# A two-layer sequence kernel: rows of B and C in 32-row groups, two Vector operations moved to GpSimd, and a new order of calls

## The reference

```
x = LN(x + gated recurrence(x))     # conv 4 taps, two gates, a scan of the log decay
                                    # clipped at -80, a scan of the state, out projection, rms norm
x = LN(x + W2 relu(W1 x + b1) + b2) # 256 -> 1024 -> 256
x = LN(x + SSM(x))                  # in projection -> x_in, z; conv 4 taps, silu;
                                    # (B, C, dt) = x_conv @ x_proj_w.T   (16 + 16 + 1 columns)
                                    # h[n] = exp(dt*A[n])*h[n] + dt*B[n]*x_conv   for 16 states n
                                    # y = sum over n of h[n]*C[n];  y*silu(z) @ out_proj_w.T
x = LN(x + W2 relu(W1 x + b1) + b2) # 16 experts of 64, which is one 256 -> 1024 -> 256
```

## Time and profile before

| | us |
|---|---|
| median of 3 runs | 961.66 |
| lowest and highest | 961.19 and 963.65 |
| the profiled execution | 961.2 |
| its span in the trace | 959.4 |

### The profile page before, as it was taken

How to read it: one execution, slowest core, us unless ns; L and a number is a source line. 1 busy time by engine, 2 the same in 40 slices (tenths; PEclk the granted TensorE clock), 3 DMA queues, 4 the chain that set the end, 5 groups by cost and what they waited for, 6 DMA issues and landing times. The chain is left out here.

```text
span 959.4 us, 9608 instructions
## 1 busy us (share of the span) xinstructions
PE 796.9 (83%) x2802; PEld 528.2 (55%) x2802; DVE 802.2 (84%) x1013; ACT 671.6 (70%) x1345; POOL 561.4 (59%) x468
## 2 busy tenths in 40 slices
PE   2385867978987799999899999998998797787585
PEld 1264644736554556475647564756476546546464
DVE  5245566677799999999999999999999999989761
ACT  4347687588767865997699769876976685465452
POOL 0202457437836793789378937893776376565421
PEclk9597977989998889999999999999999799789597
DMA  9000000000100010001000100010000000000000
GB/s 315 12 23 22 23 1 22 1 1 0 56 1 0 1 42 13 0 1 59 8 1 1 60 1 0 1 46 0 1 1 27 1 1 1 23 0 1 22 1 22
DMA packets 10341, 19.49 MB, mean 20 GB/s; under 512 B 1457, under 2 KB 5297, under 8 KB 10289
## 3 DMA queue, kind: packets, MB, share of 16 engines
q1 hardware_dynamic: 10288, 18.88, 5.8%
HBM read 14.69 MB, written 4.19 MB: 20 GB/s over the span
## 5 line engine op out<-in xcount | busy, mean ns | idle before, releaser
L385 POOL TENSOR_TENSOR y<-y,hC 128x1024 f32<-128x1024 f32 (+3 forms) x140 | 280.1, 2001 | 77.3 <-DVE hC L1461 73.4
L1914 PE MATMUL pC<-w,hT 128*128 128x256 f32 x1024 | 232.4, 382 | 4.9 <-ACT hT L754 4.9
L819 ACT ACTIVATE dA<-dt,A_neg 128x512 f32<-128x512 f32 (+3 forms) x320 | 187.5, 630 | 54.3 <-DVE hs L1450 53.8
L1914 PEld LDWEIGHTS pC<-w,hT 128*128 128x128 f32 x1024 | 194.5, 191 | 36.7 <-issue 7.2
L1450 DVE TENSOR_TENSOR_SCAN hs<-dA,carry,pS 128x512 f32<-128x512 f32 (+3 forms) x192 | 193.4, 1008 | 18.1 <-ACT dA L819 10.4
L2037 PE MATMUL pS<-stack,sel 97*128 97x512 f32 (+3 forms) x320 | 148.0, 515 | 54.5 <-DVE hs L1450 54.0
L1435 DVE TENSOR_TENSOR pS<-u,pS 128x1024 f32<-128x1024 f32 (+3 forms) x160 | 159.8, 999 | 17.4 <-PE pS L2037 16.8
L1461 DVE TENSOR_TENSOR hC<-hs,pS 128x1024 f32<-128x1024 f32 (+3 forms) x160 | 157.5, 985 | 15.3 <-PE pS L2037 15.1
L1450 DVE TENSOR_TENSOR_SCAN hs<-dA,pS 128x512 f32<-128x512 f32 (+1 forms) x128 | 138.2, 1080 | 14.6 <-POOL carry L392 6.0
L754 ACT ACTIVATE hT<-pA,ffb_sb 128x512 f32<-128x512 f32 (+3 forms) x160 | 94.7, 599 | 59.2 <-PE pA L1907 58.9
L1907 PE MATMUL pA<-tg,w 128*128 128x512 f32 (+3 forms) x320 | 127.9, 538 | 7.7 <-ACT hT L754 6.3
(11 more groups left out here) (120 smaller groups left out, 1101.5 us busy)
## 6 DMA issues: line engine op xcount, KB each, us to landing
xt<-xT SPq DMA_DIRECT2D x6, 515.0 KB, 4.7
xtok<-x SPq DMA_DIRECT2D x6, 512.0 KB, 5.3
out<-x3b SPq DMA_DIRECT2D x6, 512.0 KB, 2.9
w<-w1a SPq DMA_DIRECT2D x1, 1024.0 KB, 8.3
w<-w2a SPq DMA_DIRECT2D x1, 1024.0 KB, 10.4
w<-w1b SPq DMA_DIRECT2D x1, 1024.0 KB, 8.3
w<-w2b SPq DMA_DIRECT2D x1, 1024.0 KB, 9.9
xt<-xT SPq DMA_DIRECT2D x2, 259.0 KB, 7.8
```

The lines of the kernel that those rows point to most:

```text
L385: nc.gpsimd.tensor_tensor(y[:, :, 0:ch.T], so_far, hC[:, n % CRING, :, 0:ch.T], ALU.add).then_inc(S["y_sum"], 1)
L819: nc.scalar.activation(dA[:, k % ARING, 0:ch.T], dt[ch.side][:, h, 0:ch.T], ACT.Exp, scale=A_neg[:, h, n:n + 1]).then_inc(S["dA_ready"], 1)
L1914: mm = nc.tensor.matmul(dst[:, b * D:b * D + D], src(k, t0), w[:, k, :], start=k == 0, stop=k == nk - 1)
```

## The change

1. `x_proj` now yields 66 rows: two copies of B on partitions 0 to 31, two of C on 32 to 63, two of dt on 64 and 65. The weight for it is loaded once and laid out by three small copies on POOL (`x_proj_weights`). A column `hi_lo`, made from the identity at the start, tells on each row whether it is the rounded part or the remainder, so that `x_proj_high` and `x_proj_low` each work on all 66 rows.
2. A spread of B now multiplies 32 rows (0 to 31), one of C 32 rows (32 to 63), one of dt 2 rows. In PE's lists spread_B(n+2) and spread_C(n) stand directly next to each other nearly everywhere.
3. `decay_steps` and `readout` run on POOL. The factor 0.5 of the read-out moves into `op_w`, when it is centred.
4. All the lists of calls are in a new order. No other call is added or removed.

```diff
-                for at in (0, LO):
-                    weight("xp", xp_w[:, :, at:at + NX], xpT)
+                weight("xp", xp_in[:], xpT)
...
+            def decay_steps(ch):
+                c = ch.i
+                pool.wait_ge(S["la_scan"], 2 * c + 2)
+                nc.gpsimd.tensor_tensor(decay[:, :, 0:ch.T], st[:, 0:H, 1:1 + ch.T], st[:, 0:H, 0:ch.T], ALU.subtract).then_inc(S["dl_ready"], 1)
+
+            def readout(ch, gate):
+                if gate is not None:
+                    conv_done(pool, gate)
+                pool.wait_ge(S["y_sum"], ADDS * (ch.i + 1))
+                nc.gpsimd.tensor_tensor(yg[:, :, 0:ch.T], y[:, :, 0:ch.T], zz[ch.side][:, :, 0:ch.T], ALU.mult).then_inc(S["yg_ready"], 1)
+
+            def x_proj_weights(ch):
+
+                if ch.i == 0:
+                    pool.wait_ge(weight_loaded["xp"], 16)
+                    twice = xp_w[:, :, 0:DT_ROW].rearrange("p h (g r n) -> p h g r n", g=2, r=2)
+                    for k in range(2):
+                        nc.gpsimd.tensor_copy(twice[:, :, :, k, :], xp_in[:, :, 0:2 * NS].rearrange("p h (g n) -> p h g n", g=2)).then_inc(S["xp_ready"], 1)
+                    nc.gpsimd.tensor_copy(xp_w[:, :, DT_ROW:NXK], xp_in[:, :, 2 * NS:NX].to_broadcast([P, H, 2])).then_inc(S["xp_ready"], 1)
...
-                nc.scalar.mul(stack[ch.side][0:NXK, 0:ch.T], pA[0][0:NXK, 0:ch.T], 0.5).then_inc(S["stack_hi"], 1)
+                nc.scalar.activation(stack[ch.side][0:NXK, 0:ch.T], pA[0][0:NXK, 0:ch.T], ACT.Copy, scale=hi_lo[0:NXK, 1:2]).then_inc(S["stack_hi"], 1)
...
-                V.scalar_tensor_tensor(out=s[LO:NXK, 0:ch.T], in0=pA[0][LO:NXK, 0:ch.T], scalar=0.5, in1=s[LO:NXK, 0:ch.T].bitcast(F32),
-                                       op0=ALU.mult, op1=ALU.subtract).then_inc(S["stack_ready"], 1)
+                V.scalar_tensor_tensor(out=s[0:NXK, 0:ch.T], in0=pA[0][0:NXK, 0:ch.T], scalar=hi_lo[0:NXK, 0:1],
+                                       in1=s[0:NXK, 0:ch.T].bitcast(F32), op0=ALU.mult, op1=ALU.add).then_inc(S["stack_ready"], 1)
...
-            def spread(dst, ch, row):
-
-                return nc.tensor.matmul(dst[:, 0:ch.T], sel[0:NXK, row:row + 1].to_broadcast([NXK, P]), stack[ch.side][0:NXK, 0:ch.T],
+            def spread(dst, ch, lo, n, col):
+                return nc.tensor.matmul(dst[:, 0:ch.T], sel[lo:lo + n, col:col + 1].to_broadcast([n, P]), stack[ch.side][lo:lo + n, 0:ch.T],
                                         start=True, stop=True)
...
-                spread(pA[0], ch, 2 * NS).then_inc(S["s_mm"], 1)
+                spread(pA[0], ch, DT_ROW, 2, NS).then_inc(S["s_mm"], 1)
...
-                spread(B_bank(n), ch, n).then_inc(S["B_mm"], 1)
+                spread(B_bank(n), ch, 0, GROUP, n).then_inc(S["B_mm"], 1)
...
-                spread(C_bank(n), ch, NS + n).then_inc(S["C_mm"], 1)
+                spread(C_bank(n), ch, GROUP, GROUP, n).then_inc(S["C_mm"], 1)
```

More of the change, by code:

```diff
@@ L490, in entry @@
                 if scan is not None:
-                    save_carry(scan, 14)
                     sum_states(scan, 13)
@@ L529, in step @@
                     mconv_add(prep, 3)
+                if scan is not None:
+                    save_carry(scan, 7)
                 if gate is not None:
@@ L2129, in entry @@
                     if scan.i > 0:
-                        spread_B(scan, 2)
+                        spread_B(scan, 3)
+                if prep is not None:
+                    down(0, prep, 1, 1)
+                if gate is not None:
+                    gate_mm(gate, 1, 0)
+                if scan is not None:
+                    if scan.i > 0:
+                        spread_C(scan, 1)
+                if tail is not None:
+                    out_proj1(tail, prep)
+                if scan is not None:
+                    if scan.i > 0:
+                        spread_B(scan, 4)
+                        spread_C(scan, 2)
@@ new lines, in entry @@
+                if prep is not None:
+                    dt_row(prep)
+                if tail is not None:
+                    down(1, tail, 0, 0, gate=gate, prep=prep)
+                    down(1, tail, 0, 1)
+                if scan is not None:
+                    spread_B(scan, 13)
+                    spread_C(scan, 11)
+                if gate is not None:
+                    x1_transpose(gate, 0, prep, tail)
+                    x1_transpose(gate, 1, prep, tail)
+                if scan is not None:
+                    spread_B(scan, 14)
+                    spread_C(scan, 12)
@@ new lines, in entry, with step @@
+                if scan is not None:
+                    spread_C(scan, 14)
+                if prep is not None:
+                    spread_B(prep, 0)
+                if gate is not None:
+                    down(0, gate, 0, 0, tail=tail)
+                if scan is not None:
+                    spread_C(scan, 15)
+                if gate is not None:
+                    down(0, gate, 0, 1)
+            def step(ahead, gate, prep, scan, tail):
+                if scan is not None:
+                    spread_B(scan, 1)
+                if prep is not None:
+                    down(0, prep, 1, 0)
+                if scan is not None:
+                    spread_B(scan, 2)
+                    spread_C(scan, 0)
@@ L2151, in entry @@
                     x2_transpose(prep, 1, gate)
+                if scan is not None:
+                    spread_B(scan, 5)
+                    spread_C(scan, 3)
                 if tail is not None:
@@ L2169, in entry @@
                     up(1, tail, 1, prep)
+                if scan is not None:
+                    spread_B(scan, 7)
+                    spread_C(scan, 5)
                 if prep is not None:
+                    in_proj_z(prep, 0, tail)
                     in_proj_z(prep, 1, tail)
```

1215 lines of the change are left out of this document (571 added, 644 removed).

## The result

| | before | changed |
|---|---|---|
| median us (4 runs each) | 961.54 | 974.14 |
| lowest and highest | 961.19, 963.65 | 971.10, 978.73 |
| ratio, 95% interval | | 1.0137, 1.0095 to 1.0179 |
| profiled execution, its span | 961.2, 959.4 | 978.73, 976.9 |

What follows compares the result with a forecast made beforehand. DVE and PE together were taken to bound the late part of a step, DVE alone the early part. 961.2 - 13.2 + 6 x (0.4 - 0.25) + 1.2 + 1.5 = 951.6, 952 on the median's basis; range 944 to 974.

Steps and rivals of the forecast that it cites:

- the price of a pair: Spreads on PE: two neighbouring spreads taken at 0.23 us, against 0.43 for two now; bounds 0.22 to 1.5.
- the rival: Late part of a step, x_proj to C0: the switch costs more than the pass saved, 970 to 980 us; chance 0.20.
- the gap of over 0.5 us around a pair: Sign on PE that the forecast is wrong: a gap of over 0.5 us around each pair.
- single waits of 2 us: Sign that the forecast is wrong: DVE waits 2 us and more for spreads before output(12) and output(0).
- What leaves DVE: Read-out and difference of the decays leave DVE: 2.27 us a step of 512 tokens, 13.2 us in the bound stretch.
- What POOL gets: Two operations of 2.37 us a step on POOL, the difference starting when log_A ends, no stall; bounds nothing or 2.05 a step.
- What the new order asks of PE: Late part of a step: C12 1.2 us late, C0 1.8 at 0.43 a pair; 0.4 a step at 0.23, against 0.25 now.
- The ends: Tail +1.2 us for the last two read-outs; start +1.5, with bounds of -4 and +4.
- POOL once in each step: Rival: POOL shuts DVE out once in each step, 6 x 2.05 us on the sum, 964; chance 0.05.
- the order gains: Rival: the order gains by itself in the first 265 us, 4 to 8 us less, 945; chance 0.08.
- No more than two spreads: Rival: a pair costs 0.43 us, 1.8 late a step, +8.4, 960; chance 0.19 together with pairs in between.

Runs made afterwards that it cites:

- e10: Changed kernel (32-row spreads) with the opening and entry-step orders of before, difference of the decays placed where its input is ready; 967.88 us (1.0079).
- e8: Changed kernel with 97-row spreads and the opening and entry-step orders of before, difference of the decays placed where its input is ready; 951.57 us (0.9898).
- e5: Changed kernel, layout and order kept, each spread's matmul reading all 66 rows with zeros in the selection for the other groups; 961.43 us (0.9995).
- e3: Kernel before with only the 32-row layout of the spreads, order of before, both operations still on DVE; 976.02 us (1.0155).
- e1: Changed kernel with the 97-row layout of the spreads back, new order and move to POOL kept; 958.71 us (0.9961 of before).
- e11: 97-row spreads, old opening and entry orders, new step and closing order, with the two moved operations back on DVE; 968.86 us (1.0071).
- e7: Kernel before with only the two operations moved to POOL, decay_steps ahead of row_scales(LN_Y) in a step and of sum 2 in entry steps; 961.01 us (0.9975).
- e2: Kernel before with only the two operations moved to POOL, decay_steps queued late, behind row_scales(LN_Y) in a step; 986.45 us (1.0255).

## Why the prediction was wrong

**The step that failed** is the price of a pair: "I take 0.23, the lower end: spreads of float32r stand between float32 groups already and cost one pass, so a switch of kind is free so far". What stands in those rows is a change of the number format on the full array. It is no evidence on a change of the row group, and the trace of before had none. The pair measured 0.60 in the row shown and 0.51 in about as many others, a single spread 0.61. I had the price of the rival right for every second pair (0.62, and 0.4 more for each single), and gave it 0.20; its condition "decides from a pair of about 0.53 us on" is met by the upper level and not by the lower. For a step of the changed kernel, with 14 pairs, two singles and one cluster of three, that is at most 14 x 0.17 + 2 x 0.39 = 3.2 us more on PE, and 1.6 if all pairs stood at the lower level (0.06 more than two spreads); 1.1 to 1.7 of it reach the end in the steps between 350 and 650 us (e10 against e8). In all the layout costs 12.7 (e5), 14 (e3), 15.4 (e1) or 16.3 (e8 and e10). The rival's sum, 979, is 5 too high, and its place was off: it put 11 of its loss into the steps and 2 into the opening, while 11.7 of the 19.2 us between the traces of changed and e1 lie before the third dt_x. Of its signs the gap of over 0.5 us around a pair came; single waits of 2 us did not (1.33, 0.38 and 0.64 in the step shown).

The rule of the Trainium skill that I cited as speaking against the change (TensorEngine Tiling (Array Packing), Key Properties: changing the tiling mode drains TensorE) agrees with the runs, and its number here is 0.38 us there and back. Its other rule, that different row groups run together (TensorE: Matmul & The Clock Gate, Part 3), agrees too: two records in 0.50 us. Both hold at once, and the first is larger. The error was to weigh them as alternatives and let a row that spoke of neither decide.

**What leaves DVE** was right as busy time, 782.8 against the 782 named. As time of the kernel it depends on the lists: e11 against e8 shows 1.8 to 3.9 us a step, mostly 2.3 to 2.5, around the 2.27 of the sum, and 17.3 in all; in the old lists the move brings next to nothing (e7, 961.0). "An operation taken off DVE in this stretch shortens it" held for one of the two.

**What POOL gets**: nothing shut out DVE in the changed kernel (its twelve recurrences of 512 tokens have a mean of 1270 ns, those of before, with the one of the earlier trace rows, 1442). But the difference of the decays did not start when `log_A` had ended: `log_A` ended at 490.4 us and POOL took the difference up at 493.92, behind `row_scales(LN_Y)` and sum 2. In the changed order ACT doesn't wait for it. In e2 it has the same place in a step and ACT has its old order, and together with a late place in the entry steps that cost 25 us.

**What the new order asks of PE**: at 97 rows the walk foresaw the spread for output(12) 1.2 us late and that for output(0) 1.8, at 0.43 a pair. The places were right, the sum twice too large: the 1.8 has the 1.2 in it, and with 66 rows and 0.46 a pair DVE waits 0.27 at output(12) and 0.66 at output(0) in the step of e5 from 455.5 us on, 0.9 in all. That e8, where a pair costs two passes and the early lists are the old ones, lands on 951.6, next to the forecast's 952, is luck: pairs taken too cheap stand against lateness taken too high, and no run separates the two.

**The ends.** The tail got no longer (70.7 against 71.3; in e8 69.0), where I had added 1.2. Of the two ends the start was off most: I took +1.5 with an upper bound of 4; the changed lists of the entry steps cost 6.3 to 7.1. I counted only the operations moved there, and called what the new lists do a gain or nothing. By itself this would have made 957 of 952.

**Rivals.** POOL once in each step and "the order gains" fell. "No more than two spreads" gave 960; e5, at just that price, took 961.4, but most of the difference to 952 is the early order (7.1 by e1 and e8), not lateness in the steps, so it came near for another reason.

The sum as the runs give it, from before: the move and the new step lists -9.9 (e8), the new entry and opening lists +7.1, the layout +15.4: 961.5 + 12.6 = 974.1. Each term is a difference of two medians along one path of edits, so the sum closes of itself; another order of the edits would give other terms.

## To carry to other kernels

Price a matmul by the distance between its neighbours' starts, not by its own record: a small row group between full matmuls costs 0.38 us here, nearly two of the 0.2165 us passes, so by these rows it pays only where each visit saves two passes or more. A shorter list of one engine helped here only together with new lists of the others, and a new list is to be judged stage by stage: here one part of it, with the move, gave 10 us and another took 7. When a rule speaks against a change and the trace has no row on it, the rule keeps its weight.

## What the runs showed that I had not expected

- A matmul over 66 rows between matmuls over 128 costs one pass (0.23 us), one over 64 rows 0.59: a border between 64 and 66 rows, worth 25 us in this kernel.
- In e3, a cluster of dt's spread and a pair, three records on three row groups, stands between groups that start 3.98 us apart (518.11 and 522.09): 0.52 over their passes, no more than a pair. The price is for the visit, not for the number of matmuls in it.

```profile
518.11 3.62 PE L1943 MATMUL pC<-w,hT 128*128 128x256 f32 x16
521.66 0.50 PE L2066 MATMUL pA<-stack,sel 2*128 2x512 f32 x1
521.66 0.50 PE L2066 MATMUL pS<-stack,sel 32*128 32x512 f32 x2
522.09 3.72 PE L1943 MATMUL pC<-w,hT 128*128 128x256 f32 x16
```
